# The square of q moved from ScalarE to VectorE in a Runge-Kutta scan with a fused FFN

## The chip, the core and the metric

One core of a Trainium2 chip runs the whole kernel as one program. The metric is the device time of an execution in microseconds. Engines are TensorE (PE; its weight loads are PEld), VectorE (DVE), ScalarE (ACT), GpSimd (POOL) and SyncE (SP), which issues the transfers here. Each engine has an instruction queue of its own, worked off in order; engines wait for one another by semaphores, and an engine waits on a semaphore for a result of its own where the next instruction reads it.

## The reference

Two parts. The first is a scan over 128 time steps of a coupled system with state q and p, each 16 (batch) x 256. A step is a Runge-Kutta step of fourth order, with four derivatives one after the other:

```
def _derivative(q, p, drive, coupling, bias):
    i_couple = jnp.tanh(q) @ coupling.T
    dq = q - q ** 3 / 3.0 - p + drive + i_couple + bias
    dp = EPSILON * (q + ALPHA - BETA * p)
...
dq2, dp2 = _derivative(q + 0.5 * DT * dq1, p + 0.5 * DT * dp1, drive, coupling, bias)
...
q_next = jnp.clip(q_next, -CLAMP, CLAMP)
```

The second part runs a mixture-of-experts FFN over the q of all steps: logits by W_router, softmax, the best two of 8 experts (176 wide each), and a shared expert (704 wide) with a sigmoid gate. Experts are silu(gate) * up, then the down projection. The output is x plus the FFN's. The FFN of a step doesn't feed back into the scan.

## The kernel before

**Tiling.** Features lie on the 128 partitions, so q is a tile of 128 x 32 (two halves of the features, 16 of the batch). The 128 steps are cut into 16 blocks of 8 steps; a step has 4 stages (one per derivative), so a block has 32 stages, and the scan has 512. The FFN of block b - 1 runs beside the scan of block b, cut into pieces that are put into the stages by tables: 17 tiles of hidden features, whose up-projection is in stage UP_AT[j] (in 3 to 24, without those that leave a rest of 2 by 4), the silu on ScalarE one stage later, hidden (VectorE's product of silu and up) two stages later (HIDE_AT), POOL's multiplication with the routing weight in WEIGH_AT (13 to 29), the down-projection in DOWN_AT. The first block runs without an FFN, with weight preparation in its place (`prepare`), and behind the last block runs the last FFN alone.

**A stage** of the scan. ScalarE computes th_hi (tanh of q in 16 bits, L348), th (the same in 32 bits, L349) and square (L358), then its part of the FFN. VectorE forms th_lo = th - th_hi (L685). TensorE multiplies the coupling matrix with th_hi (8 matmuls, L449) and then with th_lo (4 matmuls, L456), then its part of the FFN, then a number of matmuls into warm_ps whose result isn't used (WARM, L537). VectorE meanwhile forms cubic from square and q (L688), force = rest - cubic (L707), and at the end of the stage q for the next stage from coup_ps and force (L720), for which it waits for TensorE (`coupled`) and for force (`forced`). With q the next stage begins.

The cube's third comes out as cubic = (square - LINEAR[k]) * q, with square = c/3 * q * q. ScalarE gets c/3 as the square root of it in its input scale:

```
SQUARE = [math.sqrt(c / 3.0) for c in C]
```

**The order on VectorE** in a stage is written out by hand in `scan_stage`. In the first of four stages (k = 0): rest from p, the clip of q_raw into q_trace (L658), prepare, the slot, base (L664), th_lo, cubic, p_sum, force, rest, q. In the others: prepare, the slot, the updates of p_sum, base or rest, th_lo, cubic, base or p_now, force, q; in the fourth stage also p_part (L623). The slot is the FFN's part of VectorE (`ffn`: routing steps, hidden L778, the finish of a block L764). In stages other than the first of four the engine waits behind the slot for its own last q (`q_ready`).

In the first of four stages q is the clipped one in q_trace, and ScalarE's square waits for the clip (`q_clipped`); its two tanh read q_raw before the clip.

Of the kernel before, what the change touches and what calls it, by code (L numbers as in the profile page):

```python
# [24 lines left out]
ALU = mybir.AluOpType  # L25
ACT = mybir.ActivationFunctionType
# [9 lines left out]
STAGES = 4 * STEPS  # L36
# [8 lines left out]
C = [0.5 * DT, 0.5 * DT, DT, DT / 6.0]  # L45
# [18 lines left out]
R4_Q2 = W3 + 2.0 * PB * PG / 3.0  # L64
R4_Q3 = 2.0 * W3 - 2.0 * PG / 3.0
assert np.float32(R3_Q1) == 1.0
SQUARE = [math.sqrt(c / 3.0) for c in C]
LINEAR = [C[0] + 1.0, C[1], C[2], C[3] + W1]
P_LOW, P_HIGH = C[0] * (-CLAMP - SHIFT), C[0] * (CLAMP - SHIFT)

# [28 lines left out]
def program(nc, x, cond, coupling, bias, w_up, w_down, w_route, identity, spread, iota, e_base, out):  # L99
    ctx = ExitStack()  # L100
    with ctx:
        def sb(name, shape, dt=F32):
            return ctx.enter_context(nc.sbuf_tensor(name, shape, dt))
# [4 lines left out]
        def sem(name):  # L108
            return ctx.enter_context(nc.semaphore(name))
# [23 lines left out]
        scale = sb("scale", [P, 2])  # L133
# [12 lines left out]
        square = sb("square", [P, KC, B])  # L146
# [59 lines left out]
        q_ready = sem("q_ready")  # L206
        q_clipped = sem("q_clipped")
        hi_ready = sem("hi_ready")
        tanh_ready = sem("tanh_ready")
        squared = sem("squared")  # L210
# [37 lines left out]
        def q0_of(i):  # L248

            return q_trace[:, :, (i - 1) % STEPS, :]  # L250
# [47 lines left out]
        def _(act):  # L298
# [39 lines left out]
            def tanh(b, st):  # L338
                if st % 4:
                    q = q_in[st % 4]  # L340
                else:
                    q = q_raw

                if isinstance(b, int) and b == 0 and st == 0:
                    act.wait_ge(in_core, 4 * 16)
                else:
                    act.wait_ge(q_ready, b * STAGES + st)
                nc.scalar.activation(th_hi[:], q[:], ACT.Tanh).then_inc(hi_ready, 1)  # L348
                nc.scalar.activation(th[:], q[:], ACT.Tanh).then_inc(tanh_ready, 1)  # L349
                if st % 4 == 0:  # L350
                    t = (b * STAGES + st) // 4
                    if t:

                        act.wait_ge(q_clipped, t)
                    q = q0_of(st // 4)
                else:
                    q = q[:]
                nc.scalar.activation(square[:], q, ACT.Square, scale=SQUARE[st % 4]).then_inc(squared, 1)  # L358

            def ffn(f, st):  # L360
                if st == 0:
# [41 lines left out]
            def one_block(b, f):  # L403
                for st in range(STAGES):
                    tanh(b, st)
                    prepare(b * STAGES + st)
                    if f is not None:
                        ffn(f, st)
# [137 lines left out]
        def _(dve):  # L546
# [51 lines left out]
            def prepare(n):  # L598

                if n == 2:  # L600
                    nc.vector.tensor_copy(ident_b[:], ident[:]).then_inc(ident_cast, 1)
                if n == MOST_AT:
                    dve.wait_ge(w_summed, W_PARTS)
                    nc.vector.reduce_sum(most[:, 1:2], w_sum[:], AX.X).then_inc(w_scaled, 1)
                if n == MOST_AT + 1:
                    dve.wait_ge(w_turned, 1)
                    nc.vector.reduce_max(most1[0:1, 1:2], route_ps[0:1, 0:P], AX.X).then_inc(w_scaled, 1)
                if n == MOST_AT + 2:
                    dve.wait_ge(w_turned, 2)
                if MOST_AT + 2 <= n < MOST_AT + 5:  # L610
                    for x in ((0, 1), (2, 3), (4,))[n - MOST_AT - 2]:
                        if x:
                            dve.wait_ge(w_scaled, x + 2)
                        power(x, 1).then_inc(w_scaled, 1)
                if LO_AT <= n < LO_AT + TILES:
                    w, w_hi, w_lo = w_tile(n - LO_AT)
                    dve.wait_ge(w_hi_ready, n - LO_AT + 1)
                    nc.vector.scalar_tensor_tensor(w_lo, w, scale[:, 1:2], w_hi, ALU.mult, ALU.subtract  # L618
                                                   ).then_inc(w_lo_ready, 1)
# [9 lines left out]
            def scan_stage(b, st, slot):  # L629

                i, k = st // 4, st % 4
                n = b * STAGES + st
                t = b * STEPS + i
                q = q_in[k][:] if k else q0_of(i)
# [23 lines left out]
                        nc.vector.tensor_scalar(q, q_raw[:], CLAMP, -CLAMP, ALU.min, ALU.max).then_inc(q_clipped, 1)  # L658
                prepare(n)
                slot()  # L660
                if k == 0:

                    dve.wait_ge(p_parted, 2 * (t + 1))
                    nc.vector.tensor_tensor(base[:], drive[:, t].rearrange("p d m b -> p d (m b)"),  # L664
                                            p_part[:, 0:3, :], ALU.subtract).then_inc(based, 1)
                else:
                    dve.wait_ge(q_ready, n)
                if k == 1:
                    update_p()

# [113 lines left out]
            def one_block(b, f):  # L784
                for st in range(STAGES):
                    def slot(st=st):
                        if f is not None:
                            ffn(f, st)
                    scan_stage(b, st, slot)
# [109 lines left out]
```

## Time and profile before

| | |
|---|---|
| median of 3 runs | 743.61 us (742.8 to 743.67) |
| the profiled execution | 745.0 us, its span 743.1 us |
| PE busy | 679.2 us (91%) |
| DVE busy | 671.2 us (90%) |
| ACT busy | 431.0 us (58%) |
| POOL busy | 174.6 us (23%) |
| mean granted clock of TensorE | 0.995 |
| square on ACT, q / q_trace | 81.7 us x384 / 29.2 us x128 |

The profile is of one execution; its own time stands 1.9 us over its span, and 0.2% over the median of the runs. Times in a timeline are microseconds from the span's start. An instruction's duration overlaps that of its neighbour on the same engine, so what an engine can do per time is read from the distance of two starts, not from the durations.

### The profile page before, as it was taken

Reading aid. Unit: us, or ns where it says so; the run is one execution under the profiler, and the core shown is the slowest. Engines: PE = TensorE matmul, PEld = TensorE weight load, DVE = VectorE, ACT = ScalarE, POOL = GpSimd, SP = SyncE. Lnnn points to the kernel's source line nnn. Section 1 sums busy time; section 2 is a strip of 40 time slices with the busy share of each in tenths; the row PEclk is TensorE's granted clock in tenths of the full one; section 3 lists DMA queues with packets and bytes.
Section 4 is the critical chain, followed back from the end, with each engine's and each line's share of the span. In section 5 each row is a group of like instructions: output and inputs, shape, how many; then the busy total and the mean of one; then the engine's idle time right before and its main releaser. Section 6 shows DMA issues by size and latency. Waiting matters only on the chain.

```text
span 743.1 us, 33477 instructions
## 1 busy us (share of the span) xinstructions
PE 679.2 (91%) x12101; PEld 601.7 (81%) x12101; DVE 671.2 (90%) x4624; ACT 431.0 (58%) x2310; POOL 174.6 (23%) x372
## 2 busy tenths in 40 slices
PE   2437999999999999999999999999999999999998
PEld 1326888888888888888888888888888989888888
DVE  5899999999999999999999999999999899999972
ACT  3865646556565655656565565656556565654643
POOL 0001221312222231222223122221312213132233
PEclk9999999999999999999999999999999999999999
DMA  8600000000000000000000000000000000000000
GB/s 319 189 2 2 3 3 11 4 9 4 10 3 3 11 3 10 4 10 4 3 11 3 11 2 11 2 4 10 4 10 4 10 4 2 11 4 10 4 9 9
DMA packets 8630, 13.64 MB, mean 18 GB/s; under 512 B 1520, under 2 KB 7984, under 8 KB 8208
## 3 DMA queue, kind: packets, MB, share of 16 engines
q1 hardware_dynamic: 8464, 11.50, 4.5%
q8 instruction: 95, 1.56, 0.9%
q14 instruction: 71, 0.58, 0.3%
HBM read 9.40 MB, written 2.10 MB: 15 GB/s over the span
## 4 chain that ended last, share of the span: by engine, by line
PE 62%; DVE 22%; issue 7%; ACT 3%; POOL 3%; DMA 2%; SPq 0%; DVEq 0%; POOLq 0%; ACTq 0%
PE up_ps L507 18%; PE down_ps L521 14%; PE coup_ps L456 12%; PE coup_ps L449 11%; PE warm_ps L537 5%; DVE th_lo L685 2%; POOL hidden L839 2%; PE route_ps L488 2%; DMA wf<-in_w_up 2%; DVE q L720 2%; DVE p_part L623 2%; DVE q_raw L720 1%; DVE w L618 1%; DVE p_sum L643 1%; DVE force L707 1%
## 5 line engine op out<-in xcount | busy, mean ns | idle before, releaser
L507 PE MATMUL up_ps<-q_hi,w 128*128 128x128 f16 x2176 | 226.5, 220 | 0.7 <-POOL q_lo L809 0.7
L449 PE MATMUL coup_ps<-th_hi,c 128*128 128x16 f16 x4096 | 183.2, 171 | 30.1 <-ACT th_hi L348 27.8
L449 PEld LDWEIGHTS coup_ps<-th_hi,c 128*128 128x128 f16 x4096 | 148.0, 97 | 71.3 <-ACT th_hi L348 48.0
L348 ACT ACTIVATE th_hi<-q 128x32 f16<-128x32 f32 x384 | 88.0, 229 | 189.0 <-DVE q L720 187.3
L507 PE MATMUL up_ps<-q_lo,w 128*128 128x128 f16 x1088 | 197.2, 220 | 0.0
L839 POOL TENSOR_TENSOR hidden<-hidden,comb_s 128x128 f32<-128x128 f32 x272 | 124.5, 459 | 295.4 <-PE coup_ps L456 274.4
L507 PEld LDWEIGHTS up_ps<-q_hi,w 128*128 128x128 f16 x2176 | 175.0, 98 | 0.8 <-POOL q_lo L809 0.8
L521 PE MATMUL down_ps<-hidden,wd 128*128 128x128 f32 x1088 | 157.8, 285 | 0.0
L456 PE MATMUL coup_ps<-th_lo,c 128*128 128x16 f16 x2048 | 132.2, 173 | 24.3 <-DVE th_lo L685 17.1
L521 PEld LDWEIGHTS down_ps<-hidden,wd 128*128 128x128 f32 x1088 | 133.3, 191 | 0.0
L456 PEld LDWEIGHTS coup_ps<-th_lo,c 128*128 128x128 f16 x2048 | 85.8, 97 | 58.5 <-DVE th_lo L685 32.5
L537 PE MATMUL warm_ps<-c 128*128 128x128 f16 x1245 | 128.3, 222 | 0.0
L720 DVE SCALAR_TENSOR_TENSOR q<-coup_ps,c_un,force 128x32 f32<-128x32 f32 x384 | 96.3, 251 | 25.3 <-PE coup_ps L456 0.9
L507 PEld LDWEIGHTS up_ps<-q_lo,w 128*128 128x128 f16 x1088 | 106.3, 98 | 0.0
L685 DVE TENSOR_TENSOR th_lo<-th,th_hi 128x32 f16<-128x32 f32 x512 | 96.5, 189 | 10.3 <-ACT th L349 4.5
L392 ACT ACTIVATE act_s<-up_ps,unscale 128x128 f32<-128x128 f32 x272 | 97.9, 361 | 5.0 <-PE up_ps L507 4.7
L778 DVE SCALAR_TENSOR_TENSOR hidden<-act_s,unscale,up_ps 128x128 f32<-128x128 f32 x272 | 92.2, 339 | 8.5 <-ACT act_s L392 8.5
L707 DVE TENSOR_TENSOR force<-rest,cubic 128x32 f32<-128x32 f32 x512 | 98.3, 192 | 0.0
L537 PEld LDWEIGHTS warm_ps<-c 128*128 128x128 f16 x1245 | 87.7, 101 | 0.5
L348 ACT ACTIVATE th_hi<-q_raw 128x32 f16<-128x32 f32 x128 | 29.3, 229 | 91.6 <-DVE q_raw L720 91.6
L349 ACT ACTIVATE th<-q 128x32 f32<-128x32 f32 x384 | 81.8, 213 | 0.0
L358 ACT ACTIVATE square<-q 128x32 f32<-128x32 f32 x384 | 81.7, 213 | 0.0
(87 smaller groups left out, 910.0 us busy)
## 6 DMA issues: line engine op xcount, KB each, us to landing
wf<-in_w_up SPq DMA_DIRECT2D x1, 4224.0 KB, 13.5
wd<-in_w_down SPq DMA_DIRECT2D x1, 2048.0 KB, 22.4
out<-out_s SPq DMA_DIRECT2D x16, 128.0 KB, 2.1
xs<-in_x SPq DMA_DIRECT2D x1, 1920.0 KB, 19.0
sel<-in_spread SPq DMA_DIRECT2D x1, 408.0 KB, 18.8
cf<-in_coupling SPq DMA_DIRECT2D x1, 256.0 KB, 2.4
xs<-in_x SPq DMA_DIRECT2D x1, 128.0 KB, 2.2
ident<-in_identity SPq DMA_DIRECT2D x1, 64.0 KB, 2.3
```

Of the source, the lines that this page charges most:

```text
L348: nc.scalar.activation(th_hi[:], q[:], ACT.Tanh).then_inc(hi_ready, 1)
L392: nc.scalar.activation(act_s[:, j % 4, :], up_ps[j % 4][:, 0:TOK], ACT.Silu, scale=unscale[:, 1:2]).then_inc(silu_ready, 1)
L449: nc.tensor.matmul(coup_ps[:, m * B:(m + 1) * B], c16[:, part, k, m * P:(m + 1) * P], th_hi[:, k, :], start=part == m == k == 0, stop=Fals ...
L456: last = nc.tensor.matmul(coup_ps[:, m * B:(m + 1) * B], c16[:, 0, k, m * P:(m + 1) * P], th_lo[:, k, :], start=False, stop=True, skip_gro ...
L507: last = nc.tensor.matmul(up_ps[j % 4][:, h * TOK:(h + 1) * TOK], w16[:, part, k, h, j * P:(j + 1) * P], q[:, k, :], start=n == 0, stop=n ...
L521: last = nc.tensor.matmul(down_ps[:, m * TOK:(m + 1) * TOK], wd[:, j, m * P:(m + 1) * P], hidden[:, j, :], start=j == m == 0, stop=j == TI ...
L537: nc.tensor.matmul(warm_ps[:, 0:P], c16[:, 0, 0, 0:P], c16[:, 0, 0, 0:P], start=True, stop=True)
L685: nc.vector.tensor_tensor(th_lo[:], th[:], th_hi[:], ALU.subtract).then_inc(lo_ready, 1)
L707: nc.vector.tensor_tensor(force[:], rest[k][:], cubic[:], ALU.subtract).then_inc(forced, 1)
L720: nc.vector.scalar_tensor_tensor(q_raw[:] if k == 3 else q_in[k + 1][:], coup_ps[:, 0:CB].rearrange("p (m b) -> p m b", m=KC), c_un[:, (0, ...
L778: nc.vector.scalar_tensor_tensor(hidden[:, j, :], act_s[:, j % 4, :], unscale[:, 1:2], up_ps[j % 4][:, TOK:2 * TOK], ALU.mult, ALU.mult).t ...
L839: nc.gpsimd.tensor_tensor(hidden[:, j, :], hidden[:, j, :], comb_s[:, j, :], ALU.mult).then_inc(weighed, 1)
```

## The change

ScalarE no longer forms square. VectorE forms it in one instruction, (q * c/3) * q, behind the slot and ahead of all that followed the slot. In the first of four stages it waits for the clip of q on the same engine; in the others the wait for q that stood behind the slot now stands ahead of square. The semaphore `squared` is still waited for ahead of cubic.

```
-SQUARE = [math.sqrt(c / 3.0) for c in C]
+THIRD = [c / 3.0 for c in C]
...
                 nc.scalar.activation(th_hi[:], q[:], ACT.Tanh).then_inc(hi_ready, 1)
                 nc.scalar.activation(th[:], q[:], ACT.Tanh).then_inc(tanh_ready, 1)
-                if st % 4 == 0:
-                    t = (b * STAGES + st) // 4
-                    if t:
-
-                        act.wait_ge(q_clipped, t)
-                    q = q0_of(st // 4)
-                else:
-                    q = q[:]
-                nc.scalar.activation(square[:], q, ACT.Square, scale=SQUARE[st % 4]).then_inc(squared, 1)
...
                 prepare(n)
                 slot()
+                if k:
+                    dve.wait_ge(q_ready, n)
+                elif t:
+                    dve.wait_ge(q_clipped, t)
+                nc.vector.scalar_tensor_tensor(square[:], q, THIRD[k], q, ALU.mult, ALU.mult).then_inc(squared, 1)
                 if k == 0:
 
                     dve.wait_ge(p_parted, 2 * (t + 1))
                     nc.vector.tensor_tensor(base[:], drive[:, t].rearrange("p d m b -> p d (m b)"),
                                             p_part[:, 0:3, :], ALU.subtract).then_inc(based, 1)
-                else:
-                    dve.wait_ge(q_ready, n)
```

How VectorE's queue reads, from the clip of a first-of-four stage with an empty slot to the th_lo of the next stage, whose slot holds a hidden instruction. Before:

```order
L658 TENSOR_SCALAR q_trace<-q_raw 128x2x16 [waits q_ready]
L664 TENSOR_TENSOR base<-drive,p_part 128x96 [waits p_parted]
L685 TENSOR_TENSOR th_lo<-th,th_hi 128x32 [waits tanh_ready]
L688 SCALAR_TENSOR_TENSOR cubic<-square,q_trace 128x32 [waits squared]
L643 SCALAR_TENSOR_TENSOR p_sum<-q_trace,p_part 128x32 [waits p_parted]
L707 TENSOR_TENSOR force<-rest,cubic 128x32 [waits cubed]
L711 SCALAR_TENSOR_TENSOR rest<-q_trace,base 128x32 [waits based]
L720 SCALAR_TENSOR_TENSOR q<-coup_ps,c_un,force 128x32 [waits coupled,forced]
L778 SCALAR_TENSOR_TENSOR hidden<-act_s,unscale,up_ps 128x128 [waits down_ready,silu_ready]
L643 SCALAR_TENSOR_TENSOR p_sum<-q,p_sum 128x32 [waits q_ready]
L671 TENSOR_TENSOR base<-base,q_trace 128x32
L685 TENSOR_TENSOR th_lo<-th,th_hi 128x32 [waits tanh_ready]
```

The same place with the change, in two pieces (line numbers are the changed kernel's). The first of four:

```order
L649 TENSOR_SCALAR q_trace<-q_raw 128x2x16 [waits q_ready]
L656 SCALAR_TENSOR_TENSOR square<-q_trace 128x32 [waits q_clipped]
L660 TENSOR_TENSOR base<-drive,p_part 128x96 [waits p_parted]
L679 TENSOR_TENSOR th_lo<-th,th_hi 128x32 [waits tanh_ready]
L682 SCALAR_TENSOR_TENSOR cubic<-square,q_trace 128x32 [waits squared]
```

and the stage behind it:

```order
L714 SCALAR_TENSOR_TENSOR q<-coup_ps,c_un,force 128x32 [waits coupled,forced]
L772 SCALAR_TENSOR_TENSOR hidden<-act_s,unscale,up_ps 128x128 [waits down_ready,silu_ready]
L656 SCALAR_TENSOR_TENSOR square<-q 128x32 [waits q_ready]
L634 SCALAR_TENSOR_TENSOR p_sum<-q,p_sum 128x32
L665 TENSOR_TENSOR base<-base,q_trace 128x32
L679 TENSOR_TENSOR th_lo<-th,th_hi 128x32 [waits tanh_ready]
```

One instruction, square, now stands ahead of base or p_sum, and so ahead of th_lo, in each of the 512 stages; in the first of four with a wait of its own. ScalarE's queue around the same two stages before:

```order
L348 ACTIVATE th_hi<-q_raw 128x32 [waits q_ready]
L349 ACTIVATE th<-q_raw 128x32
L358 ACTIVATE square<-q_trace 128x32 [waits q_clipped]
L400 COPY comb_s<-route_ps 128x128 [waits weighed,spread_ready] x2
L392 ACTIVATE act_s<-up_ps,unscale 128x128 [waits hidden_ready,up_ready]
L348 ACTIVATE th_hi<-q 128x32 [waits q_ready]
```

and with the change:

```order
L348 ACTIVATE th_hi<-q_raw 128x32 [waits q_ready]
L349 ACTIVATE th<-q_raw 128x32
L391 COPY comb_s<-route_ps 128x128 [waits weighed,spread_ready] x2
L383 ACTIVATE act_s<-up_ps,unscale 128x128 [waits hidden_ready,up_ready]
L348 ACTIVATE th_hi<-q 128x32 [waits q_ready]
```

Square and its wait are gone from ScalarE; the other instructions keep their order.

## Rows read from the trace of the kernel before

**Rows 1.** The page: the chain that ended last, share of the span by engine.

```profile
PE 62%; DVE 22%; issue 7%; ACT 3%; POOL 3%; DMA 2%; SPq 0%; DVEq 0%; POOLq 0%; ACTq 0%
```

**Rows 2.** Timeline, eighth block, stages 16 and 17: start us, duration us, instruction.

```profile
346.37 0.33 DVE L623 TENSOR_TENSOR p_part<-p_factor,p_now 128x64 f32<-128x64 f32 x1
...
346.62 0.21 ACT L349 ACTIVATE th<-q_raw 128x32 f32<-128x32 f32 x1
...
346.72 0.17 DVE L658 TENSOR_SCALAR q_trace<-q_raw 128x32 f32<-128x32 f32 x1
...
346.81 0.25 DVE L664 TENSOR_TENSOR base<-drive,p_part 128x96 f32<-128x96 f32 x1
...
346.92 0.23 ACT L358 ACTIVATE square<-q_trace 128x32 f32<-128x32 f32 x1
346.98 0.18 DVE L685 TENSOR_TENSOR th_lo<-th,th_hi 128x32 f16<-128x32 f32 x1
...
347.21 0.26 PE L456 MATMUL coup_ps<-th_lo,c 128*128 128x16 f16 x4
...
347.41 0.19 DVE L707 TENSOR_TENSOR force<-rest,cubic 128x32 f32<-128x32 f32 x1
...
347.64 0.25 DVE L720 SCALAR_TENSOR_TENSOR q<-coup_ps,c_un,force 128x32 f32<-128x32 f32 x1
...
347.92 0.23 ACT L348 ACTIVATE th_hi<-q 128x32 f16<-128x32 f32 x1 [0.18 <-DVE q L720]
...
348.06 0.21 ACT L349 ACTIVATE th<-q 128x32 f32<-128x32 f32 x1
348.06 0.18 DVE L643 SCALAR_TENSOR_TENSOR p_sum<-q,p_sum 128x32 f32<-128x32 f32 x1
348.16 0.18 DVE L671 TENSOR_TENSOR base<-base,q_trace 128x32 f32<-128x32 f32 x1
...
348.30 0.19 DVE L685 TENSOR_TENSOR th_lo<-th,th_hi 128x32 f16<-128x32 f32 x1
...
348.55 0.26 PE L456 MATMUL coup_ps<-th_lo,c 128*128 128x16 f16 x4
...
348.65 0.19 DVE L707 TENSOR_TENSOR force<-rest,cubic 128x32 f32<-128x32 f32 x1
...
348.93 0.25 DVE L720 SCALAR_TENSOR_TENSOR q<-coup_ps,c_un,force 128x32 f32<-128x32 f32 x1
```

**Rows 3.** Timeline of DVE, the same block, stage 7.

```profile
335.02 0.18 DVE L681 SCALAR_TENSOR_TENSOR rest<-q,base 128x32 f32<-128x32 f32 x1
335.13 0.18 DVE L685 TENSOR_TENSOR th_lo<-th,th_hi 128x32 f16<-128x32 f32 x1
```

**Rows 4.** Timeline, the same block, stage 14.

```profile
343.77 0.46 POOL L839 TENSOR_TENSOR hidden<-hidden,comb_s 128x128 f32<-128x128 f32 x1 [5.23 <-PE coup_ps L456]
...
343.99 0.28 DVE L675 SCALAR_TENSOR_TENSOR rest<-q,base 128x32 f32<-128x32 f32 x1
```

**Rows 5.** Timeline of DVE, the same block, stage 29.

```profile
364.36 0.19 DVE L671 TENSOR_TENSOR base<-base,q_trace 128x32 f32<-128x32 f32 x1
364.63 0.19 DVE L685 TENSOR_TENSOR th_lo<-th,th_hi 128x32 f16<-128x32 f32 x1
```

**Rows 6.** Timelines of DVE and PE, the same block, stage 19.

```profile
350.89 0.19 DVE L685 TENSOR_TENSOR th_lo<-th,th_hi 128x32 f16<-128x32 f32 x1
...
351.33 0.24 PE L456 MATMUL coup_ps<-th_lo,c 128*128 128x16 f16 x4
```

**Rows 7.** Timeline of DVE, the first block, stage 18.

```profile
37.11 0.74 DVE L618 SCALAR_TENSOR_TENSOR w<-wf,scale,w 128x512 f16<-128x512 f32 x1
```

**Rows 8.** Timeline of ACT, the first block, stage 8.

```profile
20.79 1.07 ACT L326 ACTIVATE hidden<-wf 128x1056 f32<-128x1056 f32 x1
```

**Rows 9.** Windows: us, busy times (instructions) of the engines, PEclk, DMA share, GB/s.

```profile
334.00:337.40 3.40, 3.07 (x62) 2.67 (x61) 3.28 (x24) 2.10 (x12) 0.61 (x3) 1.00 0.00 0
415.36:418.77 3.41, 3.41 (x55) 3.41 (x52) 2.88 (x23) 1.98 (x9) 1.64 (x1) 0.50 0.12 38
```

## The prediction

> **What bounds the kernel now.** I read the page's busy shares first (the table above): TensorE 91%, VectorE 90%, ScalarE 58%. So the change takes an operation from the engine with room and gives it to one without. The chain of the last work is 62% TensorE and 22% VectorE [rows 1], which would make TensorE the bound and the exchange free. That view follows an engine's queue back as long as the queue is full, and WARM keeps TensorE's queue full on purpose, so I went on to the timeline, to see which wait ends last inside a stage.
>
> An ordinary stage is stage 17 of the eighth block [rows 2]. q ends at 347.89 (347.64 + 0.25); th ends at 348.27; th_lo starts at 348.30, as soon as th is there, and ends at 348.49; TensorE, which had finished its eight matmuls with th_hi, starts the four with th_lo at 348.55 and ends them at 348.81; the next q starts at 348.93. Period 1.29 us, the latency of one loop: q, tanh, th_lo, four matmuls, q. ScalarE is never late in it: th_hi starts 0.03 us behind q's end. The second branch, square, cubic, force, ends at 348.84 (348.65 + 0.19); q could start at 348.87, so it has 0.06 us of slack. Hence the question is only: **does the new square delay th_lo?**
>
> What an instruction costs VectorE here is not its 0.18 us of duration but its distance to the next start: p_sum 348.06, base 348.16, so 0.10 us [rows 2].
>
> **The change by kinds of stages.** Going through the 32 stages of the timeline of one block, I find four kinds.
>
> *Kind A, the first of four stages (0, 4, 8, ... 28; 8 per block).* In stage 16 the clip of q starts at 346.72, base follows at 346.81, th_lo at 346.98 [rows 2]. th has been there since 346.83 (346.62 + 0.21), so th_lo here waits for VectorE's own queue. Behind the change square stands between the clip and base and waits for the clip's end, 346.89. That wait has a price in the same rows: ScalarE's square, which waits for the same clip, starts at 346.92. VectorE's square would start there, base 0.10 us later at 347.02 where it was 346.81: th_lo is 0.21 us later. Not all of it arrives: in this stage q waits now for force (347.41 + 0.19 = 347.60, q at 347.64), while the matmuls end at 347.47 and by stage 17's distance of 0.12 would allow q at 347.59. With th_lo 0.21 later the matmuls allow it at 347.80, so the stage grows by 0.16. Force follows cubic, now 0.10 behind th_lo instead of waiting for ScalarE's square, and would end by about 347.73: no longer last. Stages 0, 8 and 12, where POOL is not at work and the clip comes earlier, give 0.17 to 0.18 the same way. Stage 4 has two routing instructions behind the clip that cover the wait: 0.10. Sum of A: 0.16 x 4 + 0.17 x 3 + 0.10 = 1.25 us per block.
>
> *Kind B, VectorE's queue is full up to th_lo (1, 2, 5, 6, 7, 9, 14; 7 per block).* In stage 7 rest and th_lo start 0.11 us apart, with th there long before [rows 3]; one more such instruction ahead of them moves th_lo by 0.10. 7 x 0.10 = 0.70 us. Stage 14 belongs here: its rest takes 0.28 us instead of 0.18 beside POOL's multiplication [rows 4]; square takes its place and its stretch.
>
> *Kind C, the slot holds a hidden instruction, and th_lo waits a little for th (10, 11, 13, 15, 17, 18, 21, 22, 25, 26; 10 per block).* In stage 17 square goes to 348.06, p_sum to 348.16, base to 348.26, th_lo to 348.36 instead of 348.30: 0.06 us. 10 x 0.06 = 0.60 us. Force moves along with it (cubic stays behind th_lo), so its slack isn't used up.
>
> *Kind D, hidden anyway (3, 19, 23, 27, 29, 30, 31; 7 per block).* In stage 29 VectorE has 0.27 us between the starts of base and th_lo [rows 5], more than a square's 0.10. In stage 19 the cover is TensorE: eight matmuls of down_ps keep it until its four with th_lo start at 351.33, although th_lo was done at 351.08 [rows 6]. Without these covers each would cost 0.06 to 0.10. Price: 0.
>
> Together 2.55 us per block of 32 stages, and 15 blocks run beside an FFN: 38.3 us.
>
> **The first block** has no FFN. In stages 18 to 31 the 0.74 us of a w instruction put VectorE in kind B [rows 7]; with stages 13 and 14 that is 13 stages of other than the first of four at 0.10, and stages 0, 4, 12, 16, 20, 24, 28 of the first of four at 0.10 to 0.18, say 0.12: 2.1 us. On the other side ScalarE is the bound for seven stages, whose 1.07 us of Abs [rows 8] stand right behind square and ahead of th_hi; there a square less, 0.12 us from its start to that of the instruction behind it, comes back: minus 0.8. Net plus 1.3.
>
> **What is taken from ScalarE** brings nothing elsewhere: its th_hi always waits for q, and act_s and comb_s, which start 0.12 us earlier, are not waited for in the steady blocks. The last FFN behind the scan has no square at all and doesn't change.
>
> **Sum.** 38.3 + 1.3 = 39.6, say 40 us. The profiled execution took 745.0 us (span 743.1), so it would take 785.0; the median of the runs is 743.6, 0.2% less, so I predict **783.6 us**, 5.4% more.
>
> The square itself is an operation that the trace doesn't show on VectorE, but its nearest row is the same instruction with the same shapes and two inputs from SBUF, p_sum: 0.18 us long, 0.10 to the next start [rows 2]. Bounds: nothing for it in kinds B and C, if it slipped into gaps, leaves A and the first block, 15 x 1.25 + 1.3 = 20 us (764); its full 0.18 in A, B and C (the queue not overlapping at all behind it) makes A 0.24, B 0.18, C 0.14 a stage, 4.6 us per block, 70 us (815). I take 0.10, since all rows between instructions of this shape with no wait between them show it.
>
> **A rule weighed.** In stage 16 p_part starts while POOL is at work and takes 0.33 us [rows 2]; in stage 14 rest starts at 343.99, inside POOL's instruction from 343.77 to 344.23, and takes 0.28 [rows 4]. Undisturbed rows of rest's shape take 0.18, so such a meeting costs about 0.10, and rest ends only 0.04 behind POOL's end. The Trainium skill, SBUF — State Buffer, says of the port pair shared by VectorE and GpSimd (section on the engine side's ports) that it is an exclusive lock: a GpSimd instruction and a VectorE one with two SBUF inputs hold each other off for the whole instruction. ScalarE's square was outside of that, VectorE's isn't. By the rule square in stage 14 would start only at 344.23, 0.24 late instead of about 0.10, and 15 blocks would take 2 us more (786); by the rows they don't. The sum goes by the rows.
>
> **Rivals.**
> 1. *Collisions (4%).* If the square met POOL's multiplication in each of the 17 stages per block that have one, at 0.10 each, 1.7 x 15 = 26 us would come on top: 810. Against it: p_sum of stage 17, in whose place square would start, takes its ordinary 0.18 us [rows 2]. Only stage 14 has POOL in the way there, counted already.
> 2. *Only the clip's wait counts (8%):* kinds B and C are absorbed, 764 us. For it: TensorE has a full queue. Against it: in stage 17 TensorE sits idle ahead of its four matmuls, which start 0.06 behind th_lo's end.
> 3. *TensorE bounds, nothing changes (3%):* 744. For it the chain's 62% [rows 1]; against it stage 17, and that only stage 19 and its like show the matmuls late for another reason than th_lo.
> 4. *The clock (5%).* TensorE's granted clock fell to 0.50, 1.2 GHz, for a stretch of 3.41 us with 55 matmuls in it; a stretch as long around stage 7, at 1.00, has 62 though TensorE waited in it too [rows 9]. The mean clock of 0.995 makes that two stretches in the execution; both lie in stages 2 to 5 of a block, behind the stages in which TensorE has least to do. With more idle time there more blocks could have one. At 7 matmuls x 3.40 / 62 = 0.4 us each, one in each of the other 13 blocks gives 5 us more: 789.
> 5. *Faster (3%).* In kind A q waits for force, which waits for cubic, which waits for ScalarE's square at 346.92 + 0.23. If VectorE's square didn't delay th_lo, the stage would win back the 0.05 us by which force is last: 8 x 15 x 0.05 = 6 us, 738. It decides where square starts less than about 0.05 later than the clip's successor does today, that is if the wait for the clip's result cost nothing. Against it are the 0.20 us between the clip's start and that of whoever waits for it.
>
> **How the numbers follow.** Forecast 77%, at 784. The range takes in above it the clock's 5 us and 5 us for kind A arriving whole (0.21 a stage, 0.04 x 8 x 15), with 2 us for the first block, and below it half of kinds B and C unarrived, 10 us, and the same 2: **772 to 796**. What is left out, rivals 1, 2, 3 and 5, is 18 in 100. Within 0.2% is what a measurement of this kernel can't tell from no change. Slower 0.94, same 0.03, faster 0.03.
>
> **What would show it.** Right, if in the profile after stage 16's th_lo starts 0.74 us behind q's end (0.53 now) and its period is 1.60 for 1.44, if stage 17's th_lo starts at 0.47 (0.41 now) with a period of 1.35, and if stages 27 to 31, 28 aside, keep 1.29; ScalarE's time falls by 512 squares, some 110 us, and TensorE's idle time ahead of th_lo's matmuls grows. Wrong, if square's distance to its successor is not 0.10, if it is stretched beside POOL, or if more stretches at 0.50 stand in the clock's row.

## The result and the profile after

The changed kernel takes 786.62 us (median of 4 runs, 786.17 to 786.86) against 743.64 us: ratio 1.058, 95% interval 1.0562 to 1.0598. The forecast was 783.6 in 772 to 796. The profiled execution took 786.63 us with a span of 784.8, where the one before took 745.0 with a span of 743.1 (the execution of [rows 1]).

The page of the changed kernel: busy times, the clock, and the chain that ended last.

```profile
PE 679.7 (87%) x12101; PEld 601.9 (77%) x12101; DVE 715.2 (91%) x5136; ACT 367.6 (47%) x1798; POOL 173.7 (22%) x372
...
PEclk9999999999999999999999999999999999999999
...
DVE 58%; PE 29%; issue 8%; DMA 2%; DVEq 1%; ACT 1%; SPq 0%; POOL 0%; POOLq 0%; ACTq 0%
```

VectorE has 512 instructions and 44.0 us of busy time more, ScalarE 512 instructions less. ScalarE's busy time falls by 63.4 us (431.0 to 367.6) and not by the "some 110 us" of the prediction, which added up the durations of the squares, although neighbours on an engine overlap. The chain turned from 62% TensorE [rows 1] to 58% VectorE; TensorE's busy time is the same, so it now waits. For what, the waits say (engine, line, what it waited for, us in total, times, longest), before and after:

```profile
PEld coup_ps L456 <- DVE th_lo L685: 32.5, 107, 0.8
PE coup_ps L456 <- DVE th_lo L685: 17.1, 53, 0.7
...
PEld coup_ps L447 <- DVE th_lo L679: 82.9, 235, 1.0
PE coup_ps L447 <- DVE th_lo L679: 55.6, 189, 0.9
```

TensorE's matmuls with th_lo wait for th_lo more often and longer. This is stages 16 and 17 of the eighth block in the changed kernel, the place of [rows 2], in the timeline:

```profile
364.93 0.25 DVE L714 SCALAR_TENSOR_TENSOR q_raw<-coup_ps,c_un,force 128x32 f32<-128x32 f32 x1
365.09 0.33 DVE L614 TENSOR_TENSOR p_part<-p_factor,p_now 128x64 f32<-128x64 f32 x1
...
365.45 0.17 DVE L649 TENSOR_SCALAR q_trace<-q_raw 128x32 f32<-128x32 f32 x1
...
365.65 0.19 DVE L656 SCALAR_TENSOR_TENSOR square<-q_trace 128x32 f32<-128x32 f32 x1
365.76 0.25 DVE L660 TENSOR_TENSOR base<-drive,p_part 128x96 f32<-128x96 f32 x1
...
365.93 0.18 DVE L679 TENSOR_TENSOR th_lo<-th,th_hi 128x32 f16<-128x32 f32 x1
366.03 0.18 DVE L682 SCALAR_TENSOR_TENSOR cubic<-square,q_trace 128x32 f32<-128x32 f32 x1
...
366.17 0.26 PE L447 MATMUL coup_ps<-th_lo,c 128*128 128x16 f16 x4 [0.27 <-DVE th_lo L679]
366.25 0.19 DVE L701 TENSOR_TENSOR force<-rest,cubic 128x32 f32<-128x32 f32 x1
...
366.55 0.25 DVE L714 SCALAR_TENSOR_TENSOR q<-coup_ps,c_un,force 128x32 f32<-128x32 f32 x1
366.71 0.34 DVE L772 SCALAR_TENSOR_TENSOR hidden<-act_s,unscale,up_ps 128x128 f32<-128x128 f32 x1
...
366.96 0.21 ACT L349 ACTIVATE th<-q 128x32 f32<-128x32 f32 x1
366.97 0.18 DVE L656 SCALAR_TENSOR_TENSOR square<-q 128x32 f32<-128x32 f32 x1
367.07 0.18 DVE L634 SCALAR_TENSOR_TENSOR p_sum<-q,p_sum 128x32 f32<-128x32 f32 x1
...
367.17 0.18 DVE L665 TENSOR_TENSOR base<-base,q_trace 128x32 f32<-128x32 f32 x1
367.27 0.18 DVE L679 TENSOR_TENSOR th_lo<-th,th_hi 128x32 f16<-128x32 f32 x1
...
367.89 0.25 DVE L714 SCALAR_TENSOR_TENSOR q<-coup_ps,c_un,force 128x32 f32<-128x32 f32 x1
```

Stage 16: q_raw ends at 365.18; the clip starts at 365.45, square 0.20 behind it (365.65), th_lo 0.75 behind q_raw's end (0.74 forecast, 0.53 before), q at 366.55. The period is 366.55 - 364.93 = 1.62 us (1.60 forecast, 1.44 before). TensorE sits idle 0.27 us ahead of its four matmuls. Stage 17: q ends at 366.80, square takes p_sum's old place at 0.17, th_lo starts at 0.47, th having been there since 367.17; period 1.34 (1.35 forecast, 1.29 before).

The stages that were to cost nothing are there too. VectorE's timeline of the changed kernel, the same block, stage 29:

```profile
384.01 0.19 DVE L656 SCALAR_TENSOR_TENSOR square<-q 128x32 f32<-128x32 f32 x1
384.12 0.18 DVE L634 SCALAR_TENSOR_TENSOR p_sum<-q,p_sum 128x32 f32<-128x32 f32 x1
384.22 0.18 DVE L665 TENSOR_TENSOR base<-base,q_trace 128x32 f32<-128x32 f32 x1
384.39 0.19 DVE L679 TENSOR_TENSOR th_lo<-th,th_hi 128x32 f16<-128x32 f32 x1
```

The gap ahead of th_lo has shrunk from 0.27 [rows 5] to 0.17 us between starts and is still one; th_lo starts 0.41 us behind q's end, where it was 0.42.

### The profile page after: what moved, and what is told of

The parts are those of the page before. It is cut to its first block, busy times and chain, and to the rows that moved or that the text cites. A ratio compares the mean times of both kernels' runs of the same rounds, so it can differ in the third digit from the quotient of the medians.

```text
span 784.8 us, 33477 instructions
## 1 busy us (share of the span) xinstructions
PE 679.7 (87%) x12101; PEld 601.9 (77%) x12101; DVE 715.2 (91%) x5136; ACT 367.6 (47%) x1798; POOL 173.7 (22%) x372
## 4 chain that ended last, share of the span: by engine, by line
DVE 58%; PE 29%; issue 8%; DMA 2%; DVEq 1%; ACT 1%; SPq 0%; POOL 0%; POOLq 0%; ACTq 0%
PE coup_ps L447 9%; PE up_ps L498 8%; DVE square L656 7%; DVE hidden L772 7%; DVE th_lo L679 6%; PE down_ps L512 5%; DVE p_part L614 4%; PE coup_ps L440 4%; DVE p_sum L634 4%; DVE q L714 4%; DVE force L701 4%; DVE q_raw L714 3%; DVE cubic L682 3%; DVE base L660 3%; DMA wf<-in_w_up 2%
## 5 line engine op out<-in xcount | busy, mean ns | idle before, releaser
L440 PE MATMUL coup_ps<-th_hi,c 128*128 128x16 f16 x4096 | 183.2, 171 | 28.1 <-ACT th_hi L348 23.3
L383 ACT ACTIVATE act_s<-up_ps,unscale 128x128 f32<-128x128 f32 x272 | 99.8, 368 | 6.4 <-PE up_ps L498 6.2
L679 DVE TENSOR_TENSOR th_lo<-th,th_hi 128x32 f16<-128x32 f32 x512 | 94.5, 185 | 2.3 <-ACT th L349 2.3
L656 DVE SCALAR_TENSOR_TENSOR square<-q 128x32 f32<-128x32 f32 x384 | 72.2, 188 | 2.4
```

The costliest lines, as they stand in the source:

```text
L440: nc.tensor.matmul(coup_ps[:, m * B:(m + 1) * B], c16[:, part, k, m * P:(m + 1) * P], th_hi[:, k, :], start=part == m == k == 0, stop=Fals ...
L656: nc.vector.scalar_tensor_tensor(square[:], q, THIRD[k], q, ALU.mult, ALU.mult).then_inc(squared, 1)
L679: nc.vector.tensor_tensor(th_lo[:], th[:], th_hi[:], ALU.subtract).then_inc(lo_ready, 1)
```

## The experiments

Each kernel was timed against the kernel before on the same chip; the table has medians in us.

| kernel | time | kernel before | difference | ratio, 95% interval |
|---|---|---|---|---|
| the change | 786.62 | 743.64 | +43.0 | 1.0562 to 1.0598 |
| e1_first_only | 767.16 | 743.86 | +23.3 | 1.0299 to 1.0334 |
| e2_others_only | 765.59 | 743.86 | +21.7 | 1.0275 to 1.031 |
| e3_both | 787.54 | 743.86 | +43.7 | 1.0578 to 1.0613 |
| e4_behind_base | 773.53 | 743.86 | +29.7 | 1.0383 to 1.0418 |
| e5_no_square | 740.16 | 743.48 | -3.3 | 0.9943 to 0.997 |
| e6_one_part | 736.37 | 743.48 | -7.1 | 0.989 to 0.992 |
| e7_gap | 739.06 | 743.48 | -4.4 | 0.9929 to 0.9956 |
| e8_behind_th_lo | 828.04 | 744.23 | +83.8 | 1.111 to 1.115 |
| e9_first_behind_base | 753.73 | 744.23 | +9.5 | 1.0113 to 1.0154 |

**The two halves of the change apart.** e1 forms square on VectorE in the first of four stages (k = 0) alone:

```
                 slot()
                 if k == 0:
+                    if t:
+                        dve.wait_ge(q_clipped, t)
+                    nc.vector.scalar_tensor_tensor(square[:], q, THIRD[k], q, ALU.mult, ALU.mult).then_inc(squared, 1)
```

> VectorE forms square only in the first of four stages; in the others ScalarE does, as before. Theory (each square delays th_lo by what it takes of VectorE's queue; kind A pays the clip's wait too): kind A alone, 19 us in the blocks with an FFN and about 1 us in the first, 744 + 20 = 764 us. Rival that the wait for the clip is all of the loss: 786. Rival that a busy VectorE loses everywhere else and the first of four are absorbed: 744 to 748. Periods by theory: stage 16 at 1.62, stages 17 and 7 as in the kernel before (1.29, 1.63).

e2 does it in the other three:

```
                 else:
                     dve.wait_ge(q_ready, n)
+                    nc.vector.scalar_tensor_tensor(square[:], q, THIRD[k], q, ALU.mult, ALU.mult).then_inc(squared, 1)
```

> The counterpart: VectorE forms square in the three other stages, ScalarE in the first of four. Theory: kinds B and C, 22 us in the blocks with an FFN, and about 0.5 us in the first: 744 + 23 = 767 us; this and the kernel with the first of four only add up to the whole loss of 43. Rival of the absorbed kinds B and C (only the clip's wait counts): 744. Periods by theory: stage 7 at 1.73, stage 17 at 1.35, stage 16 at 1.44 as before, stages 29 to 31 at 1.29.

Measured: +23.3 and +21.7, together 45.0 where the whole change has 43.0; the 2 us between them are of the size of the stops treated below, of which e1 and e2 each have their own. So neither half is absorbed, and each of the rivals, that all of the loss is the clip's wait or that all of it lies elsewhere, falls by some 20 us. Going through the stages of the two traces, e1 lengthens kind A by 1.31 us per block, e2 kinds B and C by 0.81 and 0.63, and each leaves the periods of the other kinds alone up to 0.2 us per block.

**The place in VectorE's queue alone.** e3 leaves ScalarE its square and lets VectorE form a second one, into a tile `twice` that nothing reads:

```
+                if k:
+                    dve.wait_ge(q_ready, n)
+                elif t:
+                    dve.wait_ge(q_clipped, t)
+                nc.vector.scalar_tensor_tensor(twice[:], q, THIRD[k], q, ALU.mult, ALU.mult)
```

> ScalarE keeps its square and the semaphore; VectorE forms a second square at the place of the change, with the same waits, into a tile that nothing reads. The output is the reference's. Theory (the whole loss is the place in VectorE's queue, and ScalarE's relief gives next to nothing): as the changed kernel or up to 1 us more, since the first block's seven stages with ScalarE as the bound lose their 0.12 us again: 787 us. Rival (ScalarE's relief gave something back that the sum didn't see, or the semaphore squared matters): above 790 or below 783.

Measured: 787.54 us, 0.9 more than the change; each against its own runs of the kernel before, the difference is 0.7 and the intervals overlap. So the whole loss comes from the instruction and its wait on VectorE. Whether ScalarE's relief gives back the forecast 0.8 us of the first block, the times can't tell; in the traces the first block is 0.4 us longer in e3 than in the change.

**No square.** e5 leaves ScalarE's square out and gives VectorE none; the tile stays zero, so that a term of the derivative is missing.

```
-                nc.scalar.activation(square[:], q, ACT.Square, scale=SQUARE[st % 4]).then_inc(squared, 1)
...
+                if k == 0 and t:
+                    dve.wait_ge(q_clipped, t)
-                dve.wait_ge(squared, n + 1)
```

> The kernel before without any square: ScalarE's instruction is left out, VectorE has none either, the tile square stays at zero, so the cube's third is missing from the output and only the time is read. This is the most that relieving ScalarE can give. Theory: in the first of four stages force is no longer last, minus 0.05 us in four and 0.04 in three of the eight per block, 5 us, and minus 1 in the first block: 738 us. Rival (ScalarE's work is hidden altogether): 743 to 744. Rival (ScalarE's share of 58% matters more widely): below 735.

Measured: 740.16, 3.3 us less than the kernel before, where 5 to 6 were expected. In its trace kind A is 0.31 us per block shorter, as in the fifth rival of the prediction, and kinds B, C and D are unchanged but for 0.03; the first block is 1.2 us shorter. That makes 0.31 x 15 + 1.2 = 5.9 us, against which stand some 2 us more of single long stages, treated below. That is all there was to gain from ScalarE.

**The clip's wait.** e4 is the changed kernel with square behind base in the first of four stages:

```
                                             p_part[:, 0:3, :], ALU.subtract).then_inc(based, 1)
+                    if t:
+                        dve.wait_ge(q_clipped, t)
+                    nc.vector.scalar_tensor_tensor(square[:], q, THIRD[k], q, ALU.mult, ALU.mult).then_inc(squared, 1)
```

> The changed kernel with one edit: in the first of four stages square (and its wait for the clip) stands behind base instead of ahead of it. Base doesn't need the clip and covers most of its latency. Theory: th_lo of stage 16 starts 0.62 to 0.64 behind q's end instead of 0.75, its period falls from 1.62 to 1.49; 0.12 us in each of 128 stages, 15 us: 772 us. Rival (the loss in these stages is from the number of instructions ahead of th_lo, not from the wait): unchanged, 786 to 787.

Measured: 773.53, 13.1 us less than the change. e4's timeline of VectorE, eighth block, stage 16:

```profile
359.48 0.25 DVE L715 SCALAR_TENSOR_TENSOR q_raw<-coup_ps,c_un,force 128x32 f32<-128x32 f32 x1
...
360.00 0.17 DVE L649 TENSOR_SCALAR q_trace<-q_raw 128x32 f32<-128x32 f32 x1
360.09 0.24 DVE L658 TENSOR_TENSOR base<-drive,p_part 128x96 f32<-128x96 f32 x1
360.26 0.18 DVE L662 SCALAR_TENSOR_TENSOR square<-q_trace 128x32 f32<-128x32 f32 x1
360.36 0.18 DVE L680 TENSOR_TENSOR th_lo<-th,th_hi 128x32 f16<-128x32 f32 x1
...
360.97 0.25 DVE L715 SCALAR_TENSOR_TENSOR q<-coup_ps,c_un,force 128x32 f32<-128x32 f32 x1
```

Base starts 0.09 behind the clip and covers its latency; the wait in front of square holds nothing up. th_lo starts 0.63 behind q_raw's end, period 1.49. So of the 0.21 us by which th_lo was late in these stages, half is the instruction and half the wait for the clip. e9 joins this place with e1:

> VectorE forms square in the first of four stages only, and there behind base (the two single edits together). Theory: what is left of kind A without the clip's wait, 0.42 us per block as measured in the changed kernel with square behind base, 6.3 us, and under 1 us in the first block: 750.5 us. Rival (what the edits give depends on one another): off that by more than 3 us.

Its edit is e1's with the three lines behind base. Measured: 753.73, +9.5 us where +6.9 was expected. That is 3.2 us over the expected time and so just over the 3 us that the expectation gave its rival, that the edits depend on one another. Two other readings speak against that rival: e1 less e9 is 23.3 - 9.5 = 13.8 us, about the change less e4 (43.0 - 29.7 = 13.3, each against its own runs of the kernel before), and kind A costs 0.41 us per block in e9's trace for 0.42 in e4's. Where the 3 us lie is treated below.

**The second branch.** e8 puts square, in the three other stages, behind th_lo:

```
                 nc.vector.tensor_tensor(th_lo[:], th[:], th_hi[:], ALU.subtract).then_inc(lo_ready, 1)
+                if k:
+                    nc.vector.scalar_tensor_tensor(square[:], q, THIRD[k], q, ALU.mult, ALU.mult).then_inc(squared, 1)
 
                 dve.wait_ge(squared, n + 1)
```

> The changed kernel, with square in the three other stages put directly behind th_lo and so directly ahead of cubic, which reads it. Theory (two branches, and the second has 0.06 us of slack): th_lo goes back to 0.41 in stage 17, but cubic now waits for the square's end, 0.42 + 0.10 + 0.18 + 0.03 = 0.73 behind q's end, force starts at 0.95 and q, now held by force, at 1.18: period 1.43 against 1.35 in the changed kernel and 1.29 before. Stages 27, 29, 30, 31, which cost nothing in the changed kernel, go from 1.29 to 1.43, stage 7 from 1.73 to 1.77. Sum 0.08 x 10 + 0.03 x 7 + 0.14 x 5 = 1.7 us per block, 25 us: 811 us. Rival (only th_lo's place counts, the second branch has room for a square): kinds B and C are free again, 765 us.

Measured: 828.04, the worst of all, and 17 us over the expectation. Stages 17 and 29 do what was expected, 1.45 for 1.43 us. Most of the rest is in four of the last of four stages, 15, 19, 23 and 27, which take 1.74 us, 0.27 to 0.31 more than expected. e8's timeline, eighth block, stage 27:

```profile
399.91 0.25 DVE L717 SCALAR_TENSOR_TENSOR q<-coup_ps,c_un,force 128x32 f32<-128x32 f32 x1
...
400.58 0.19 DVE L680 TENSOR_TENSOR th_lo<-th,th_hi 128x32 f16<-128x32 f32 x1
400.69 0.19 DVE L682 SCALAR_TENSOR_TENSOR square<-q 128x32 f32<-128x32 f32 x1
400.91 0.19 DVE L685 SCALAR_TENSOR_TENSOR cubic<-square,q 128x32 f32<-128x32 f32 x1
...
401.13 0.19 DVE L704 TENSOR_TENSOR force<-rest,cubic 128x32 f32<-128x32 f32 x1
401.17 0.48 POOL L836 TENSOR_TENSOR hidden<-hidden,comb_s 128x128 f32<-128x128 f32 x1 [0.98 <-PE coup_ps L447]
401.24 0.48 DVE L614 TENSOR_TENSOR p_part<-p_factor,p_now 128x64 f32<-128x64 f32 x1
401.64 0.24 DVE L717 SCALAR_TENSOR_TENSOR q_raw<-coup_ps,c_un,force 128x32 f32<-128x32 f32 x1
401.81 0.21 DVE L614 TENSOR_TENSOR p_part<-p_factor,p_now 128x64 f32<-128x64 f32 x1
```

th_lo is early again (0.42 behind q's end), but square to cubic costs 0.22 us, since cubic reads what stands directly ahead of it; with force ending at 401.32, q_raw could start at 401.35, the period of 1.43 that was expected. Then p_part, which used to start ahead of POOL's multiplication, starts 0.07 us behind POOL's start, takes 0.48 us instead of 0.22 and ends at 401.72, 0.07 behind POOL's end (401.65). q_raw stands behind it in the queue and starts at 401.64: period 1.73 instead of 1.43. That is the collision of the prediction's first rival, at another instruction and at nearly three times the price that I had given it. A part comes back: the second p_part (401.81) no longer meets POOL and takes 0.21 us instead of 0.33, and the first of four stages behind these four take 1.49 to 1.50 us for the change's 1.62; that about balances the 0.02 to 0.07 us by which many other stages are over. The clock, the prediction's fourth rival, shows here too: with more idle time on TensorE, e8's trace has eight stretches of 3.41 us at 1.2 GHz, for two before.

**What the analysis points to.** In the kernel before, th_lo of the first of four stages waits for VectorE's queue. e6 keeps square on ScalarE and clears that queue: p_part is formed in one instruction in the stage ahead.

```
-                nc.vector.tensor_tensor(p_part[:, x:x + 2], p_factor[:, x:x + 2], p_now[:].rearrange(
-                    "p m b -> p (m b)").unsqueeze(1).to_broadcast([P, 2, CB]), ALU.mult).then_inc(p_parted, 1)
+                nc.vector.tensor_tensor(p_part[:], p_factor[:], p_now[:].rearrange(
+                    "p m b -> p (m b)").unsqueeze(1).to_broadcast([P, 4, CB]), ALU.mult).then_inc(p_parted, 1)
...
-                if k == 3 and t + 1 < T:
-                    parts_of_p(2)
```

> Not the change, but what its analysis points to: in the first of four stages th_lo waits for VectorE's own queue already in the kernel before. ScalarE keeps square. The two instructions that form p_part become one of 128 columns at the place of the first, so none is left between q_raw and the clip; rest goes into the shadow of q_raw, clip and base follow. Theory: th_lo of the first of four starts 0.42 behind q's end (0.53 and 0.42 now) and force ends before the matmuls allow q: periods of stages 16, 20, 24, 28 fall from 1.44 to 1.29 or 1.30, of 0, 8, 12 from 1.33 to 1.29, while six of the stages ahead of them grow by 0.03 for the longer p_part. Net 0.75 us per block: 732 us. Rival (the bound is elsewhere and th_lo's place in the queue is not what counts): 743 or more.

Measured: 736.37, ratio 0.9905: faster than both kernels, though 4 us over the expectation. The expected periods came (stage 20 has 1.31 for 1.44), and the blocks as their median stages have them are 0.76 us shorter, 43.51 to 42.76, for 0.75 expected; the rest is in single stages that take longer, below. e7 adds VectorE's square for the first of four stages, behind base:

> The same reordering, and in addition VectorE forms square in the first of four stages only, behind base, in the gap that VectorE then has ahead of th_lo (0.30 to 0.42 behind q's end). Theory: a square in a gap costs nothing; the same time as the reordering alone, 732, within 2 us. Rival (a square on VectorE costs its 0.10 us wherever it stands, for instance by the wait for the clip): 128 x 0.10 = 13 us more, 745.

Measured: 739.06, 2.7 us more than e6: neither free nor 13 us. By the median stages e7 costs 0.30 us per block more, 4.5 us in all; against that, its trace has 3.8 us less in single long stages, treated below, and the two profiled executions are 1.4 us apart. e7's timelines of VectorE in the eighth block show both answers; stage 8:

```profile
333.20 0.18 DVE L651 TENSOR_SCALAR q_trace<-q_raw 128x32 f32<-128x32 f32 x1
333.30 0.25 DVE L657 TENSOR_TENSOR base<-drive,p_part 128x96 f32<-128x96 f32 x1
333.46 0.18 DVE L661 SCALAR_TENSOR_TENSOR square<-q_trace 128x32 f32<-128x32 f32 x1
333.58 0.19 DVE L681 TENSOR_TENSOR th_lo<-th,th_hi 128x32 f16<-128x32 f32 x1
```

and stage 20:

```profile
348.73 0.25 DVE L716 SCALAR_TENSOR_TENSOR q_raw<-coup_ps,c_un,force 128x32 f32<-128x32 f32 x1
348.89 0.30 DVE L645 TENSOR_TENSOR rest<-drive,p_now 128x32 f32<-128x32 f32 x1
349.11 0.17 DVE L651 TENSOR_SCALAR q_trace<-q_raw 128x32 f32<-128x32 f32 x1
349.20 0.25 DVE L657 TENSOR_TENSOR base<-drive,p_part 128x96 f32<-128x96 f32 x1
349.37 0.18 DVE L661 SCALAR_TENSOR_TENSOR square<-q_trace 128x32 f32<-128x32 f32 x1
349.47 0.18 DVE L681 TENSOR_TENSOR th_lo<-th,th_hi 128x32 f16<-128x32 f32 x1
```

In stage 8 q_raw ends at 333.16 (332.92 + 0.24 in the same view), square fits into the gap and th_lo starts at 0.42, its old place: the period is 1.28 and square is free. In stage 20 rest meets POOL and takes 0.30 for 0.18, the gap is gone before square comes, and th_lo starts at 0.49 behind q_raw's end (348.98), where e6 has it at 0.42. So a square in a gap is free, but in five of the eight stages (4, 16, 20, 24, 28) the gap wasn't where I had put it: their periods are 0.04 to 0.11 us longer than e6's, those of stages 0, 8 and 12 the same.

## Why the prediction was right, and where its sizes were off

**The bound.** That th_lo's start, not TensorE's queue, sets the period was the point on which all hung, and against the chain's 62% TensorE. e3 shows it: an edit that touches only VectorE's queue has the whole loss. e1 and e2 show it by the kinds of stages forecast, and e6 in the other direction: with th_lo earlier the kernel is faster. The chain moved to VectorE when the change had put it clearly last.

**The kinds.** From the periods of all stages in the two profiled executions, per block of the 15 with an FFN:

| | forecast | change | alone, in e1 or e2 |
|---|---|---|---|
| kind A | 1.25 | 1.29 | 1.31 (e1) |
| kind B | 0.70 | 0.82 | 0.81 (e2) |
| kind C | 0.60 | 0.66 | 0.63 (e2) |
| kind D | 0 | -0.03 | 0.00 (e2) |

Together 2.74 us per block for 2.55 forecast, 41.1 us for 38.3; the first block with what is ahead of it gave 0.6 for 1.3. The span grew by 41.7 us, 39.6 forecast. The first block's terms were 0.7 us too large together, and ScalarE's saved time was overstated; neither weighs much in the sum. The square's distance to its successor is the forecast's 0.10 (366.97 to 367.07 above); the 0.20 us from the clip's start to who waits for it carried over from ScalarE to VectorE unchanged.

**Off by size, first:** single stages take 0.05 to 0.35 us longer than the median of the same stage in the other blocks. Summed over blocks 3 to 16 that is 1.6 us before and 4.7 after, 5.6 in e6, 1.8 in e7. Taking the median stages alone, the change costs 45.97 - 43.51 = 2.46 us per block, just under the forecast, and kinds B and C cost 0.70 and 0.55. One of the long stages in the changed kernel, ninth block, stage 25; the bracket gives VectorE's idle time and what ended it:

```profile
424.28 0.25 DVE L714 SCALAR_TENSOR_TENSOR q<-coup_ps,c_un,force 128x32 f32<-128x32 f32 x1
424.75 0.35 DVE L772 SCALAR_TENSOR_TENSOR hidden<-act_s,unscale,up_ps 128x128 f32<-128x128 f32 x1 [0.22 <-issue]
```

VectorE was idle for 0.22 us without waiting for anything that the profile shows, and th_lo came that much later. Such stops are not scattered. Number all of VectorE's records in a trace in order, its sequencer's (waits, branches and the like) included: in the scan beside the FFN the eleven traces have 70 stops of 0.12 to 0.35 us without a wait, and every one stands at a record whose number, divided by 128, leaves 63 or 64. The change, e3, e4 and e8 have as many VectorE instructions (5136), and their long stops fall on the same stages, as far as they have them; e1 and e9 (4752) share another set. An added instruction shifts where the stops fall, and whether one delays th_lo is chance. No run moved the stops alone, so this cause is read from the traces and not tried. Of the change's 4.7 us, 3.3 lie in stages at these places and most of the rest in stages 2 to 5, where TensorE's granted clock falls to 1.2 GHz: the mean clock is 0.993 for 0.995 before, one stretch of 3.41 us more. e9 and e6 have 4.3 and 5.6 us of longer single stages, 2.7 and 4.0 more than the kernel before; by about so much, 3 to 4 us, they missed their expectations.

**Off by size, second:** "the median of the runs is 743.6, 0.2% less" scaled the forecast down by 1.4 us. The profiled execution of the kernel before was a slower one than the median; that of the changed kernel was at its median, 786.63. The working's 785.0 was the better number for the latter.

**The rule weighed.** The prediction put a meeting of VectorE and POOL at "about 0.10". That was the size of two rows in which VectorE's instruction started late in POOL's. e8 shows one that starts at POOL's beginning: 0.48 us instead of 0.22, ending 0.07 behind POOL's end. The other rows have nearly the same end: rest of stage 14 ends 0.04 behind POOL's [rows 4], and p_part of stage 16 0.08 behind it (346.70 [rows 2], POOL's instruction there ending at 346.62). The same holds for every stretched row in the eleven traces, 60 to 75 in each: the instruction takes as much longer as is left of POOL's when it starts, less 0.14 us (0.24 - 0.14 = 0.10 in stage 14, 0.41 - 0.14 = 0.27 in e8, where 0.26 was measured), and one that starts in the last 0.14 us isn't stretched. So the price of such a meeting is no fixed 0.10. The Trainium skill's rule in SBUF — State Buffer (section on the engine side's ports), that the two exclude one another for the whole instruction, describes this better than my reading of the rows did; only a whole further duration of VectorE's instruction behind POOL's end, as I had worked out by it, isn't there. In the change itself no new meeting came about (square in stage 17 takes 0.18, and the trace has 73 stretched rows for 74 before; 14 of them are squares, in the place of rest in stage 14), so the first rival fell for the reason given, and only its price was wrong.

**The rivals.** Absorbed B and C: fell by e2. TensorE as the bound: fell, by the 43.0 us. The clock: one stretch more, not thirteen; it was one of the prediction's signs of being wrong, and at 0.4 us it carries nothing. The faster one: its mechanism exists, and e5 shows its size, 0.31 us per block in kind A; but a square on VectorE costs more than that even where the clip's wait is covered (e9, +9.5).

## What to carry to other kernels

In a loop that is bound by latency, an instruction's price is what it moves the start of the one instruction that others wait for: nothing in a gap ahead of it, its distance to the next start (0.10 us here, not its duration of 0.18) in a full queue, and another 0.11, 0.21 in all, where it waits for a result of the instruction directly ahead. Busy shares and the chain couldn't tell these apart; the start of that one instruction, stage by stage, could, and showed also where there was time to gain (e6). Before a VectorE instruction with two inputs from SBUF is moved, look where POOL works: one that started well inside POOL's multiplication ended only 0.04 to 0.08 us behind it. And a difference of a few us between two kernels of this length can lie in where VectorE's stops fall.

## What the runs showed of the hardware that wasn't expected

A VectorE instruction with two SBUF inputs that starts 0.07 us behind a POOL multiplication of 0.48 us took 0.48 us itself instead of 0.22, and ended 0.07 behind it; in all traces the added time is what is left of POOL's instruction less 0.14 us.

VectorE stops for 0.12 to 0.35 us without a wait, in the eleven traces 70 times, only at places 128 of its records apart (63 or 64 beyond a multiple of 128) and with an 8192-byte packet on an instruction queue within 1 us. Most of these places cost no time in a stage; which do changes with the number of VectorE's instructions.
